# Sums over keys in one block of strips, and dense rows of eight heads in the rotary attention

## The reference

```python
# causal attention: 16 heads of 8 channels over the sequence's own 128 tokens, slopes on the distance
bias = where(pos[:, None] >= pos[None, :], -slopes[:, None, None] * rel, -inf)
attn = softmax(einsum('bhtd,bhsd->bhts', q, k) * 8 ** -0.5 + bias)
out = einsum('bhts,bhsd->bhtd', attn, v)          # then out @ Wo.T + bo
# rotary cross attention: 16 heads of 8 channels over 77 context rows
q = apply_rope(rms_norm(x @ Wq.T));  k = apply_rope(rms_norm(context @ Wk.T));  v = context @ Wv.T
attn = softmax(einsum('bhtd,bhsd->bhts', q, k) * 8 ** -0.5)
out = einsum('bhts,bhsd->bhtd', attn, v)          # then out @ Wo.T
x = layernorm(x + out)
```

## Time and profile before

| what | us |
|---|---|
| median of 3 runs | 2772.31 |
| lowest, highest of them | 2766.38, 4171.66 |
| the profiled execution | 2773.75 |
| its span, first to last instruction | 2772.0 |
| PE busy in it | 2534.0 (91%) |
| DVE, ACT, POOL busy | 1904.9, 1671.0, 1694.9 |

### The profile page before, as it was taken

The page is one execution under the profiler, slowest core; times in us unless marked ns, Lnnn a source line. Parts: engine busy times, 40 slices in busy tenths (PEclk is TensorE's granted clock), DMA queues, the critical chain, the costliest instruction groups (busy, mean ns, idle before and its releaser), DMA issues. The chain is left out here.

```text
span 2772.0 us, 61590 instructions
## 1 busy us (share of the span) xinstructions
PE 2534.0 (91%) x19168; PEld 1864.5 (67%) x19168; DVE 1904.9 (69%) x5298; ACT 1671.0 (60%) x4543; POOL 1694.9 (61%) x2110
## 2 busy tenths in 40 slices
PE   8998999999999289996999999969999999699996
PEld 6665887877877289993555555547766666458993
DVE  6884677787777355555777777765788886445655
ACT  6773666666665234444766666639888887623334
POOL 3442334555555645554888888846688887724675
PEclk9998999999999699998999999979999999899998
DMA  8932467777774122214100000000011010011336
GB/s 260 338 107 68 151 215 226 234 224 224 223 220 129 54 65 71 72 58 129 58 11 9 9 11 9 7 25 13 16 30 30 30 30 17 30 30 54 93 93 194
DMA packets 274799, 267.86 MB, mean 97 GB/s; under 512 B 30060, under 2 KB 253561, under 8 KB 274096
## 3 DMA queue, kind: packets, MB, share of 16 engines
q1 hardware_dynamic: 256912, 228.42, 27.2%
q0 software_dynamic: 17280, 34.13, 3.6%
q10 hardware_dynamic: 288, 1.38, 0.2%
HBM read 101.24 MB, written 151.85 MB: 91 GB/s over the span
## 5 line engine op out<-in xcount | busy, mean ns | idle before, releaser
L779 POOL TENSOR_TENSOR wide_probs<-wide_exps,wide_inv_sum 128x616 f32<-128x616 f32 x128 | 168.3, 1315 | 305.6 <-DVE wide_inv_sum L1580 293.0
L749 POOL TENSOR_TENSOR causal_exps<-causal_biased,causal_neg_max 128x512 f32<-128x512 f32 x256 | 262.8, 1036 | 76.4 <-DVE causal_neg_max L1594 76.2
L758 POOL DMA_INDIRECT sorted_x<-send,place_i x240 | 244.1, 1017 | 84.2 <-ACT send L1233 44.0
L1289 ACT ACTIVATE rotary_exps<-banks,rotary_neg_max 128x77 f32<-128x77 f32 x1024 | 248.7, 341 | 19.3 <-DVE rotary_neg_max L1594 19.1
L1764 POOL DMA_INDIRECT results<-gelu_tile_out,gelu_dest_i x142 | 140.1, 986 | 142.2 <-DVE gelu_tile_out L1920 120.0
L1539 DVE TENSOR_TENSOR causal_biased<-banks,regions 128x512 f32<-128x512 f32 x256 | 163.6, 680 | 80.7 <-PE banks L1115 80.4
L1764 POOL DMA_INDIRECT results<-swiglu_tile_out,swiglu_dest_i x142 | 144.6, 1019 | 116.7 <-DVE swiglu_tile_out L1915 59.4
L1833 ACT ACTIVATE gelu_hidden<-banks,gelu_slot 128x256 f32<-128x256 f32 x284 | 116.6, 470 | 159.5 <-PE banks L2010 159.4
L1258 ACT ACTIVATE causal_exps<-causal_exps 128x512 f32<-128x512 f32 x256 | 161.2, 630 | 71.4 <-POOL causal_exps L749 71.4
L1594 DVE TENSOR_REDUCE rotary_neg_max<-banks 128x4 f32<-128x308 f32 x256 | 121.7, 475 | 113.5 <-PE banks L1129 105.1
L1273 ACT ACTIVATE causal_probsT<-banks 128x512 f32<-128x512 f32 x256 | 151.6, 592 | 79.3 <-PE banks L1140 79.3
(11 more groups left out here) (385 smaller groups left out, 7018.3 us busy)
## 6 DMA issues: line engine op xcount, KB each, us to landing
v_dram<-wide_staged SPq DMA_DIRECT2D x38, 1024.0 KB, 4.4
sorted_x<-blank SPq DMA_DIRECT2D x1, 34848.0 KB, 116.8
sorted_x<-blank SPq DMA_DIRECT2D x24, 1452.0 KB, 8.7
wide_folded<-v_dram SPq DMA_DIRECT2D x128, 256.0 KB
gelu_tile_in<-sorted_x SPq DMA_DIRECT2D x71, 132.0 KB, 2.1
swiglu_tile_in<-sorted_x SPq DMA_DIRECT2D x71, 132.0 KB, 2.1
gelu_back<-results SPq DMA_DIRECT2D x16, 512.0 KB, 8.0
swiglu_back<-results SPq DMA_DIRECT2D x16, 512.0 KB, 5.4
```

What stands on the lines that cost most here:

```text
L749: pool.tensor_tensor(exps[:, (NU * pair.c + m) % ES], biased[:, m % BS].rearrange("p (h n) -> p h n", h=HU), neg_max[:, m % SLOTS].unsquee ...
L758: pool.indirect_dma_start(route["sorted_x"], bass.IndirectOffsetOnAxis(ap=r_place_i[:, b % 2, which, n // 2:n // 2 + 1], axis=0), send[:, ...
L779: pool.tensor_tensor(probs[:, half % SLOTS, 0:HH * NK].rearrange("p (k h) -> p h k", h=HH), exps[:, half % EB], inv_sum[:, half % SLOTS].u ...
L1289: last = act.activation(exps[:, (NU * c.c + k) % ES, h], scores[:, h * NK:(h + 1) * NK], ACT.Exp, bias=neg_max[:, k % SLOTS, h:h + 1])
```

## The change

In the causal stage PE makes the sums of two units in one block, on even k, straight after the scores (`late_sums`, `PLAG` 5): eight products where two blocks had four each. `probsT` has four slots for it. The values' product moves from k = 3 to k = 4, and the division of the first sequence from k = 4 to k = 5 (`DIVIDE_AT`).

In the rotary stage the exponentials of two units, eight heads of 77 keys, stand one behind the other in 616 columns, padded with zeros to 640. PE turns them in five transposes of 128 columns (two for an even unit, three for an odd one) and ACT copies 256 and 384 columns. A column block then holds keys of one or more heads, so the values have to lie in the same order over the partitions: ACT copies the product of the values into `v_rows` (one buffer, as a third part of the early pair, at k = 7); SP stores it to DRAM in four DMAs and loads it back in five, in the dense order, into `v_dense` (two buffers). `dense_sum` makes eight products for two units, on one k in two. The early pair's next copy into `v_rows` waits for the stores of the pair before (`v_stored`). `ctxT` has four slots instead of eight, and `residual`, which the rotary stage did not use, goes.

```diff
@@ -650,9 +658,34 @@
-            def step(f, ahead=None, pair=None):
+            def store_values(pair):
+                sp.wait_ge(early_done, pair.count(EARLY, EARLY))
+                rows = route["v_dram"][4 * HALF_ROWS * pair.c:4 * HALF_ROWS * (pair.c + 1)].rearrange("(m h k) c -> h k m c", h=4, k=NK)
+                for h in range(4):
+                    sp.dma_start(rows[h], v_rows[0:NK].rearrange("k (m r) -> k m r", r=PITCH)[:, :, 64 * h:64 * h + 64]
+                                 ).then_inc(v_stored, 16)
+
+            def load_values(pair):
+                s = pair.c % 2
+                sp.wait_ge(v_stored, 16 * 4 * (pair.c + 1))
+                if pair.c >= 2:
+                    sp.wait_ge(pv_done, pair.back(2).count(NU, NU))
+                for b in range(2):
+                    for n in range(2):
+                        at = HALF_ROWS * (2 * (2 * pair.c + b) + n)
+                        sp.dma_start(v_dense[:, s, b, n, 0:4], route["v_dram"][at:at + 512].rearrange("(c p) d -> p c d", p=P)).then_inc(v_loaded[s], 16)
+                rows = route["v_dram"][2 * HALF_ROWS * 2 * pair.c:2 * HALF_ROWS * 2 * (pair.c + 1)].rearrange("(m r) d -> r m d", m=4)
+                sp.dma_start(v_dense[0:HALF_ROWS - 512, s, :, :, 4].rearrange("p b n d -> p (b n) d"), rows[512:HALF_ROWS]).then_inc(v_loaded[s], 16)
+
+            def step(f, ahead=None, pair=None, *behind):
                 if f is not None:
                     load(f)
+                if kind == "rotary" and pair is not None:
+                    store_values(pair)
+                if kind == "rotary" and behind[2] is not None:
+                    if behind[2].c == 0:
+                        sp.wait_ge(ready, READY)
+                    load_values(behind[2])
                 if kind == "wide" and pair is not None:
@@ -667,12 +700,14 @@
                 if kind != "causal":
-                    sp.dma_start(ctxT[:, s, :, 0:NK], ctxT_dram[:, bass.ds(f.index(2), 2), :]).then_inc(x_loaded[s], 16)
+                    if kind == "rotary" and f.c >= CTX:
+                        sp.wait_ge(early_done, f.back(CTX).count(EARLY, EARLY))
+                    sp.dma_start(ctxT[:, f.c % CTX, :, 0:NK], ctxT_dram[:, bass.ds(f.index(2), 2), :]).then_inc(x_loaded[s], 16)
                 if f.c == min(6, n_pairs - 1):
...
-            run_steps(sp, step, n_pairs, 3 if kind == "wide" else 1, 4)
+            run_steps(sp, step, n_pairs, {"wide": 3, "causal": 1, "rotary": 6}[kind], 4)
@@ -884,8 +926,11 @@
                 return act.activation(qk_sq[:].rearrange("p n h d -> p (n h d)"), f_bank, ACT.Square)
-            if m == 3:
-                return act.activation(value_heads(s2)[0:NK, :, :, 0:D], f_bank[0:NK, 0:2 * P].rearrange("p (g x d) -> p g x d", g=4, x=8), copy)
+            if m == 4:
+                if f.c >= 1:
+                    act.wait_ge(v_stored, 16 * 4 * f.c)
+                return act.activation(v_rows[0:NK].rearrange("p (m w) -> p m w", w=PITCH // 4)[:, :, 0:D],
+                                      chip.banks[0:NK, 6, 0:2 * P].rearrange("p (m d) -> p m d", d=D), copy)
             if f.back(2).real:
@@ -897,11 +942,13 @@
         FRONT_AT = {"wide": [(0, 0), (1, 0), (2, 0), (3, 0), (4, 0), (5, 0), (7, 0)],
-                    "causal": [(0, 0), (1, 0), (2, 0), (3, 1)], "rotary": [(5, 0), (7, 0)]}[kind]
-        EARLY_AT = [(0, 0), (1, 0)]
-        LATE = (2, 3)
-
-        TLAG, PLAG, OLAG = {"wide": (4, 5, 6), "causal": (3, 4, 5), "rotary": (2, 3, 4)}[kind]
+                    "causal": [(0, 0), (1, 0), (2, 0), (4, 1)], "rotary": [(5, 0)]}[kind]
+        EARLY_AT = [(0, 0), (1, 0), (7, 0)]
+        EARLY_PARTS = (0, 1, 4)
+        LATE = (2,)
+
+        TLAG, PLAG, OLAG = {"wide": (4, 5, 6), "causal": (3, 5, 5), "rotary": (2, 3, 4)}[kind]
+        DIVIDE_AT = (5, 6) if kind == "causal" else (4, 6)
         Z_AT = 5
@@ -983,7 +1030,12 @@
                                 pe.wait_ge(front_done, e.back(LEAD + 1).count(FU, FU))
-                        front_pe(pe, e, m).then_inc(early_ps, 1)
+                        if m == 2 and e.c >= LEAD:
+                            pe.wait_ge(turn_done, e.count(TURNS, TURNS))
+                            pe.wait_ge(front_done, e.back(LEAD).count(FU, FU))
+                        if m == 2 and e.c >= LEAD + 2:
+                            pe.wait_ge(norm_done, 2 * (e.c - LEAD - 1))
+                        front_pe(pe, e, EARLY_PARTS[m]).then_inc(early_ps, 1)
@@ -1027,19 +1080,34 @@
-            def late_sum(pair, n):
-                b, j = divmod(n, UB)
-                g, odd = divmod(j, 2)
+            def late_sums(pair, n):
+                b, g = n // UB, n % UB // 2
                 pe.wait_ge(probsT_done, pair.count(NU, n + 1))
-                if n == 0:
+                if n == 1:
                     pe.wait_ge(front_done, pair.count(FU, FU))
-                if j == 0 and pair.back(1).real:
+                if n % UB == 1 and pair.back(1).real:
                     pe.wait_ge(o_done, pair.back(1).count(2, b + 1))
-                for h in range(HU):
-                    strip = 272 * 2 * b + 256 * odd + 32 * (4 * g + h)
-                    last = pe.matmul(o_bank[b][32 * h:32 * h + 32, g * P:(g + 1) * P], values[0:NK, pair.c % 2, strip:strip + 32],
-                                     probsT[0:NK, n % 2, h * P:(h + 1) * P], start=odd == 0, stop=odd == 1)
-                last.then_inc(pv_done, 1)
+                for odd in range(2):
+                    for h in range(HU):
+                        strip = 272 * 2 * b + 256 * odd + 32 * (4 * g + h)
+                        last = pe.matmul(o_bank[b][32 * h:32 * h + 32, g * P:(g + 1) * P], values[:, pair.c % 2, strip:strip + 32],
+                                         probsT[:, (n - 1 + odd) % 4, h * P:(h + 1) * P], start=odd == 0, stop=odd == 1)
+                last.then_inc(pv_done, 2)
+
+            def dense_sum(pair, n):
+                b, g, s = n // UB, n // 2 % 2, pair.c % 2
+                pe.wait_ge(probsT_done, pair.count(NU, n + 1))
+                if n == 1:
+                    pe.wait_ge(v_loaded[s], 16 * 5 * (pair.c // 2 + 1))
+                if n % UB == 1 and pair.back(1).real:
+                    pe.wait_ge(o_done, pair.back(1).count(2, b + 1))
+                for second in range(2):
+                    for strip in range(4):
+                        chunk = strip + second
+                        last = pe.matmul(o_bank[b][32 * strip:32 * strip + 32, g * P:(g + 1) * P],
+                                         v_dense[:, s, b, g, chunk, 32 * (strip % 2):32 * (strip % 2) + 32],
+                                         probsT[:, (NU * pair.c + n) // 2 % 2, chunk * P:(chunk + 1) * P], start=second == 0, stop=second == 1)
+                last.then_inc(pv_done, 2)
@@ -1127,6 +1195,9 @@
                             pe.matmul(s_bank[k % 2][:, 0:HU * NK], q, moving, start=True, stop=True).then_inc(s_ps, 1)
+                    at = lagged(c, u, k, PLAG)
+                    if kind == "causal" and at is not None and k % 2 == 0:
+                        late_sums(*at)
                     at = lagged(c, u, k, TLAG)
@@ -1136,20 +1207,25 @@
                             pe.wait_ge(probsT_done, bc.count(NU, bk + 1))
-                        for h in range(HU):
-                            last = pe.transpose(p_bank[n % 2][0:NK, h * P:(h + 1) * P], exps[:, (NU * pair.c + n) % ES, h], ident)
+                        if kind == "rotary":
+                            for m in range(3 if n % 2 else 2):
+                                at = (2 * (n % 2) + m) * P
+                                last = pe.transpose(p_bank[n % 2][:, m * P:(m + 1) * P], exps[:, (NU * pair.c + n) // 2 % 2, at:at + P], ident)
+                        else:
+                            for h in range(HU):
+                                last = pe.transpose(p_bank[n % 2][0:NK, h * P:(h + 1) * P], exps[:, (NU * pair.c + n) % ES, h], ident)
                         last.then_inc(probsT_ps, 1)
...
                         front(f, k, 0)
-                    if late and u is not None and k in (4, 6):
-                        turn_back(u, (k - 4) // 2)
+                    if late and u is not None and k in DIVIDE_AT:
+                        turn_back(u, DIVIDE_AT.index(k))
                     at = lagged(c, u, k, PLAG)
...
                         weighted_sum(*at)
-                    if at is not None and late:
-                        late_sum(*at)
+                    if at is not None and kind == "rotary" and at[1] % 2 == 1:
+                        dense_sum(*at)
                     if f is not None:
@@ -1267,10 +1343,17 @@
                         act.wait_ge(probsT_ps, pair.count(NU, n + 1))
-                        if before(pair, n, 2) is not None:
-                            bc, bk = before(pair, n, 2)
-                            act.wait_ge(pv_done, bc.count(NU, bk + 1))
```

(48 more changed lines are left out.)

38 lines of the change are left out of this document (26 added, 12 removed).

## The result

The changed kernel takes 2791.32 us (median of 7 runs, 2783.76 to 2793.08) against 2772.31: a ratio of 1.0074, interval 1.0057 to 1.0091. The ratio leaves out two much longer runs of the kernel before, 2941.77 and 4171.66 us. It is slower by 19 us where I forecast 61 less, and outside my range. The profiled execution has a span of 2787.8 us, 15.8 more than before.

The account below looks back on a forecast made before the run. PE bounds plain rotary pairs; causal pairs are PE's part, then DVE's chain. 2773.75 - 39 (causal) - 36 (rotary steady) + 14 (opening) = 2712.75 us profiled, so 2711; range 2675 to 2765, the forecast's own 2690 to 2732 (chance 0.48).

Parts of the forecast that it names:

- still under DVE's 7.31: Causal pair, scores of k = 4 to the output's turn: PE needs some 6.3 us, DVE's chain stays 7.31.
- The first part: Causal pair, scores of k = 0 to those of k = 4: PE sets the pace, 8.38 us shrinks to about 7.1.
- 13.60 still fits: Causal pair: POOL's 13.60 us of busy time fits in the forecast pair of 14.8 us.
- (d): Rival: nothing eats the gain; plain rotary pairs 13.6 us, opening +7, causal -45, so 2679 us; chance 0.14.
- (e): Rival: the block of sixteen sums costs 0.72 us; causal -30, rotary -25, opening +14, so 2731 us; chance 0.08.
- (b): Rival: the rotary values' store to DRAM lands late in each pair; 2744 us; chance 0.24.
- (c): Rival: the store lands late at a higher row price, 55 ns and eleven engines; about 2905 us; chance 0.06.
- Rotary, steady: Rotary stage's steady pairs: fewer transposes, sum blocks and copies gain 36 us, bounds 15 and 58; plain pairs 14.0 us.
- the clock that I had priced at 4 us: Rotary pairs with routing: longer idle PE lowers the next pair's granted clock, in three of six fours, +4 us.
- The opening: First rotary pairs: each early step waits for the store of the step before, +14 us (+7 to +40).
- the store: Rotary values to DRAM: 0.5 us issue, 2.2 landing, rows at 30 ns; 8.5 us taken, bracket 7.3 to 9.4.
- my upper figure: Rotary values' store: 77 partitions go by sevens to eleven engines, 224 rows per engine, 9.4 us.

Follow-up runs that it names:

- e3: Changed kernel with the causal normalise that writes X one k later on DVE (k 6 and 7): 2790.74 us, ratio 1.0076.
- e4: Changed kernel with the causal divisions back at k 4 and 6 and the values' product between them at k 5: 2755.85 us, ratio 0.994.
- e12: Changed kernel with POOL's causal residual, variance and rstd at k 2, X written by ACT and its shift made by POOL: 2724.04 us, ratio 0.9832.
- e11: Changed kernel with each pair's rotary values stored twice to DRAM, the copy into v_rows waiting for both: 2802.01 us, ratio 1.013.
- e9: Changed kernel, causal divisions at k 4 and 6, POOL's statistics at k 2, X on ACT, DVE keeping a two-column product: 2740.77 us, ratio 0.9905.

## Why the prediction was wrong

**The step that failed** is in the causal part: "still under DVE's 7.31, which the change leaves as it was: the division of the first sequence one k later is the same work in the same chain". It failed twice. The chain held two instructions that POOL sets, X by its length and the sixth maximum by its start (e3), so it does not simply start earlier when PE's scores do: that takes 0.94 (e4). And the division was what had stood between the fifth maximum and X; one k later X stands directly behind the maximum, waits, and then meets the next instructions of POOL: the pair is 1.0 longer than in e4. I had seen DVE "without idle" and took that for work of its own. With the block of sixteen the 7.3 that I wrote down is reached only where POOL's statistics come early and X has left DVE (7.23 in e12).

**The first part**: forecast 7.1, measured 7.48. The block saved what I had counted. What I missed is a new wait of 0.40 us: the keys' product now comes before ACT has copied xT (row 1441.85 above).

**POOL's "13.60 still fits"** was the wrong question. POOL had room in sum; its place within the pair counted. None of my rivals had this mechanism: (d) and (e) varied PE's gain, (b) and (c) the transfers.

**Rotary, steady**: right in kind, 18 to 26 for 36. Plain pairs take 14.35 to 14.48 (forecast 14.0) with PE busy for 13.8 (forecast 13.4). Four fours in the middle gave 8.4 in all, where I had 4.4 each less some clock. The rows above show why for the first of a four: DVE is busy for 17.82 of 18.54, and the earlier trace rows had 17.52 of 18.24; the change takes nothing from DVE. I had forecast 0.3 less there, and it takes 0.3 more. For the second and third I have no run that tells what holds them; that stays open. Of the clock that I had priced at 4 us little came: one such pair, at a granted clock of 0.82, took 19.15 for 18.54.

**The opening**: +2.4 for +14. The term that I mis-sized is the store, and I counted one wait too many. ACT's copies after:

```profile
1877.91 0.38 ACT L932 ACTIVATE rotary_v_rows<-banks 77x256 f32<-77x256 f32 x1 [1.22 <-PE banks L894]
...
1883.46 0.38 ACT L932 ACTIVATE rotary_v_rows<-banks 77x256 f32<-77x256 f32 x1 [1.92 <-DMA v_rows<-rotary_v_rows]
...
1888.81 0.38 ACT L932 ACTIVATE rotary_v_rows<-banks 77x256 f32<-77x256 f32 x1 [1.86 <-DMA v_rows<-rotary_v_rows]
...
1894.32 0.38 ACT L932 ACTIVATE rotary_v_rows<-banks 77x256 f32<-77x256 f32 x1 [2.04 <-DMA v_rows<-rotary_v_rows]
...
1903.98 0.38 ACT L932 ACTIVATE rotary_v_rows<-banks 77x256 f32<-77x256 f32 x1 [1.29 <-PE banks L894]
```

From the end of a copy to the next it is 5.0 to 5.2 us, not 8.5, and steps are 5.3 to 5.6 apart, not 9. The fifth copy waits for PE and not for a store; it comes 26.1 behind the first, where I had 36. In e11, whose stores take as long as I had put it (8.6 to 9.4), the opening is 13.5 longer than before the change (81.3 for 67.8), near my 14, so the mechanism held in the main and its sizes did not. DMA traffic of a plain pair after, packets and then the queue's packets, MB and share:

```profile
DMA packets 5467, 1.50 MB, mean 100 GB/s; under 512 B 5337, under 2 KB 5465, under 8 KB 5465
...
q1 hardware_dynamic: 5465, 1.47, 44.2%
```

and of one before:

```profile
DMA packets 417, 0.23 MB, mean 14 GB/s; under 512 B 288, under 2 KB 416, under 8 KB 416
...
q1 hardware_dynamic: 416, 0.21, 5.3%
```

44.2% of 16 engines for 15 us are 106 us; 5.3% for 15.7 are 13. The difference is 93 us for 5049 packets, 18 ns each where I took 30. The packets also tell how many engines a store had. Before, 288 packets less 256 rows of the context leave 32 small ones for two loads, 16 each. After, 5337 less 4928 rows of values and 256 of the context leave 153. Less the same 32 these are 121 = 4 x 11 + 4 x 16 + 13, where sixteen for each of the nine new DMAs would make 144. Read as one small packet for each engine that takes part, which no run shows by itself, a store of 77 partitions had eleven engines, and the last load, of 104, thirteen. Then a store is 224 rows per engine at 18 ns, 4.0 us, about what the second store adds in e11 (3.7 to 4.3), and issue and landing are the other 1.0 to 1.2, where I had 2.7. So the engines were those of my upper figure; the price of a row and the fixed part were too high. The Trainium skill, "DMA: Bandwidth & Descriptors", Specifications, has reading, modifying and writing below 512 bytes; at 18 ns for 256 bytes, against 25 for the scattered 528, no doubling shows. Rival (b) was far away for the same reason, and e11 bounds it: even 9 us fit.

## What to carry to other kernels

An engine without idle time is not an engine with work of its own: before a chain is carried over unchanged, compare the lengths of each of its instructions with the shortest of its kind in the trace, and where one varies, look for what ends with it on DVE's and POOL's timelines. When the fullest engine is relieved, ask for each instruction of the next chain what else it is tied to, and how long after the last common point that comes. And a step that is moved changes its neighbours: what stood between two others may have been the cover of a wait.

## What of the hardware was not expected

The length of one instruction of DVE was set by another engine. The view of the tile X after groups the same normalise by stage (shortest, median and longest in ns):

```profile
L1658 DVE TENSOR_SCALAR X<-wide_z,wide_mean_var,wide_rstd x64: 330/340/584, 310.8 to 927.1; 128x128 f32<-128x128 f32 x64
L1658 DVE TENSOR_SCALAR X<-causal_z,causal_mean_var,causal_rstd x64: 337/889/1065, 1345.7 to 1865.3; 128x128 f32<-128x128 f32 x64
```

With no instruction of POOL beside it X takes 0.34 us; beside them the median is 0.89, and in e9 an instruction of 128x2 took 0.87 in place of 0.15. The trace books this as busy time of DVE, not as a wait, so no view of waits names POOL. Rows of 256 bytes to and from DRAM cost 18 ns of packet time each.
